# One gate in four of the expert steps moved from VectorE to GpSimd, with two passes of ScalarE to prepare it

## The reference, cut to what matters

```
xn = layernorm(x)                                     # x: 4096 rows of 256
s  = state_space_block(xn)                            # conv, silu, scan over the 4096 rows, 128 x 64 states
tok_w = softmax over the 2 best of 8 experts, per row
g, u = xn @ w1[e], xn @ w3[e]                         # 256 -> 1024, per expert e
hid  = silu(g) * u
out  = sum over the 2 chosen experts of tok_w * (hid @ w2[e])     # 1024 -> 256
y    = x + s * silu(out)
```

## Time and profile before

| | |
|---|---|
| time, median of 3 runs | 1337.58 us (1336.42 to 1339.75) |
| the profiled execution's own time | 1342.63 us |
| its span | 1340.8 us |
| pair loop, first to last scan | 124.4 us to about 1299.8 us of the span |
| busy: TensorE, VectorE, GpSimd, ScalarE | 89%, 87%, 80%, 56% of the span |
| mean granted TensorE clock | 0.945 of full speed |

### The profile page before, as it was taken

One profiled execution on the slowest core, in us unless ns is written; L12 is line 12 of the kernel. 1 busy time (PEld: TensorE's weight loads), 2 busy tenths in 40 slices (PEclk: granted clock), 3 DMA queues, 4 the chain that ended last, 5 costly groups with the idle time before them and its releaser, 6 DMA issues.

```text
span 1340.8 us, 26192 instructions
## 1 busy us (share of the span) xinstructions
PE 1194.0 (89%) x7740; PEld 921.7 (69%) x7740; DVE 1168.6 (87%) x1675; ACT 756.1 (56%) x1619; POOL 1076.3 (80%) x1042
## 2 busy tenths in 40 slices
PE   6788999999999999998999998998899988999760
PEld 5455777777777777776777776876677867777530
DVE  7795989988899989897899888997888988999988
ACT  3754675556554665466555754556455664545642
POOL 0043889888998988888998897898888987989994
PEclk8889999999999999999999999999999999999655
DMA  7124446553557445643574457443754456465658
GB/s 230 52 86 119 135 134 174 169 193 121 161 148 222 134 145 161 220 138 112 168 234 130 135 161 224 135 130 112 214 171 134 132 171 209 142 181 177 181 184 282
DMA packets 124319, 216.55 MB, mean 162 GB/s; under 512 B 15040, under 2 KB 40768, under 8 KB 124160
## 3 DMA queue, kind: packets, MB, share of 16 engines
q10 hardware_dynamic: 73728, 134.25, 34.4%
q1 hardware_dynamic: 43616, 61.83, 14.0%
q0 software_dynamic: 6816, 18.62, 4.4%
HBM read 190.67 MB, written 23.99 MB: 160 GB/s over the span
## 4 chain that ended last, share of the span: by engine, by line
PE 60%; POOL 11%; DVE 10%; issue 8%; DMA 6%; ACT 3%; SPq 1%; ACTq 1%; DVEq 0%; POOLq 0%
PE bank L1323 28%; PE bank L1293 13%; PE bank L1271 7%; PE bank L1339 6%; POOL arena L440 5%; DMA wring<-in_w_all 4%; POOL hid L455 2%; DVE arena L1045 2%; ACT th L720 1%; PE bank L1173 1%; DVE arena L983 1%; PE bank L1198 1%; DVE arena L1036 1%; PE bank L1306 1%; DVE arena L871 1%
## 5 line engine op out<-in xcount | busy, mean ns | idle before, releaser
L440 POOL TENSOR_TENSOR arena<-arena,c_rep 128x512 f32<-128x512 f32 x512 | 604.3, 1186 | 109.3 <-DVE arena L1045 97.8
L1045 DVE TENSOR_TENSOR_SCAN arena<-bank,carry,arena 128x512 f32<-128x512 f32 x512 | 653.1, 1276 | 16.7 <-ACT bank L807 16.5
L1323 PEld LDWEIGHTS bank<-xgT,wring 128*128 128x128 f32 x4288 | 524.4, 196 | 122.8 <-issue 78.4
L1323 PE MATMUL bank<-xgT,wring 128*128 128x128 f32 x4288 | 544.3, 281 | 42.4 <-DMA wring<-in_w_all 18.4
L807 ACT ACTIVATE bank<-arena,a_neg 128x512 f32<-128x512 f32 x512 | 354.8, 693 | 103.1 <-DVE arena L1045 41.1
L1036 DVE TENSOR_TENSOR arena<-bank,b_rep 128x512 f32<-128x512 f32 x512 | 352.4, 688 | 32.1 <-PE bank L1339 10.5
L720 ACT ACTIVATE th<-bank 128x256 f32<-128x256 f32 x284 | 109.1, 384 | 346.7 <-PE bank L1323 321.3
L1293 PE MATMUL bank<-wring,hid 128*128 128x256 f32 x1072 | 273.0, 386 | 15.9 <-POOL hid L455 15.8
L1339 PE MATMUL bank<-stack,pick 128*128 128x512 f32 x512 | 273.3, 538 | 8.4 <-DVE arena L1036 8.4
L1293 PEld LDWEIGHTS bank<-wring,hid 128*128 128x128 f32 x1072 | 194.4, 191 | 74.9 <-POOL hid L455 34.6
L455 POOL TENSOR_TENSOR hid<-gt,ue 128x256 f32<-128x256 f32 x284 | 207.1, 729 | 21.5 <-DVE gt L1057 16.4
(11 more groups left out here) (181 smaller groups left out, 760.4 us busy)
## 6 DMA issues: line engine op xcount, KB each, us to landing
arena<-delta_d ACTq DMA_DIRECT2D x512, 256.0 KB, 3.7
wring<-in_w_all SPq DMA_DIRECT2D x64, 384.0 KB, 6.0
xn<-in_x SPq DMA_DIRECT2D x4, 1024.0 KB, 9.6
xn_d<-xn SPq DMA_DIRECT2D x4, 1024.0 KB, 4.7
parts_d<-spare SPq DMA_DIRECT2D x16, 256.0 KB, 4.1
stack<-parts_d SPq DMA_DIRECT2D x16, 256.0 KB, 6.2
wring<-results SPq DMA_DIRECT2D x8, 512.0 KB, 8.1
arena<-results SPq DMA_DIRECT2D x8, 512.0 KB, 8.5
```

The costliest lines, as they stand in the source:

```text
L440: pool.tensor_tensor(p_ring[:, s % P_RING, :], h_ring[:, s % H_RING, :], of_chunk(c_rep, c, 2), ALU.mult).then_inc(s_hc, 1)
L1045: v.tensor_tensor_scan(out=h_ring[:, s % H_RING, :], data0=a_bank[s % 2][:, :], data1=b_ring[:, s % B_RING, :], initial=carry[:, q:q + 1], ...
L1323: ins = pe.matmul(bank[:, m * SW + r * SLOT:m * SW + (r + 1) * SLOT], wring[:, 2 * j + r, (2 * m + h) * P:(2 * m + h + 1) * P], xgT[:, i % ...
```

## The change

The fourth step of every tile (`POOLED` = 3; 71 of the 284 steps) gets its gate from GpSimd. GpSimd can't read the PSUM bank here, so ScalarE first writes two things to SBUF behind its tanh and copy: the gate half of the bank, copied into `gt`, and tanh + 1, written over `th` in place. Then it raises `s_gc`. GpSimd waits for `s_gc`, multiplies `th` and `gt` into `gt`, raises `s_gp`, and, after waiting for its own result, makes `hid` as before. VectorE skips this step's gate. ScalarE's next tanh (the next tile's first step) now waits for `s_gp`, and TensorE's reuse of the bank waits for `s_gc`.

```diff
+POOLED = STEPS - 1
+        def gated(eng, k):
+            if k % STEPS == POOLED:
+                eng.wait_ge(s_gp, k // STEPS + 1)
+            else:
+                eng.wait_ge(s_gt, (STEPS - 1) * (k // STEPS) + k % STEPS + 1)
...
             def hidden(i, j):
                 k = STEPS * i + j
-                pool.wait_ge(s_gt, k + 1)
+                if j == POOLED:
+                    pool.wait_ge(s_gc, i + 1)
+                    pool.tensor_tensor(gt[:, k % 2, :], th[:, :], gt[:, k % 2, :], ALU.mult).then_inc(s_gp, 1)
+                gated(pool, k)
                 pool.wait_ge(s_ue, k + 1)
...
                 act.wait_ge(s_gu, k + 1)
-                ge(act, s_gt, k)
+                if k:
+                    gated(act, k - 1)
                 act.activation(th[:, :], bank[:, 0:SW], ACT.Tanh, scale=0.5).then_inc(s_th, 1)
                 ge(act, s_hid, k - 1)
                 act.activation(ue[:, k % 2, :], bank[:, SW:2 * SW], ACT.Copy).then_inc(s_ue, 1)
+                if j == POOLED:
+                    act.activation(gt[:, k % 2, :], bank[:, 0:SW], ACT.Copy)
+                    act.wait_ge(s_th, k + 1)
+                    act.activation(th[:, :], th[:, :], ACT.Identity, bias=1.0).then_inc(s_gc, 1)
...
-                    if turn == "step":
+                    if turn == "step" and j != POOLED:
                         k = STEPS * i + j
                         v.wait_ge(s_th, k + 1)
...
                 if kind == "step":
-                    pe.wait_ge(s_gt, STEPS * t + k + 1)
+                    if k == POOLED:
+                        pe.wait_ge(s_gc, t + 1)
+                    else:
+                        gated(pe, STEPS * t + k)
```

More of the change, by code:

```diff
@@ L285, in mamba_and_experts @@
         s_gu, s_xgT, s_th, s_gt, s_ue, s_hid = (sem(k) for k in ("s_gu", "s_xgT", "s_th", "s_gt", "s_ue", "s_hid"))
-        s_o, s_oev = sem("s_o"), sem("s_oev")
+        s_o, s_oev, s_gc, s_gp = sem("s_o"), sem("s_oev"), sem("s_gc"), sem("s_gp")
         s_res = sem("s_res")
```

## The result

The changed kernel takes 1375.57 us (1373.82 to 1377.44), the kernel before 1338.66 us beside it: ratio 1.0276, 95% interval 1.0258 to 1.0294, or 36.9 us slower. The sign was forecast, the size was not: 11 us were expected, and the time lies above the stated range. The profiled execution took 1374.88 us, with a span of 1373.1 us.

A forecast was written before the change was run, and what follows sets the result against it. It took the chain that ended last, 60% TensorE and 11% GpSimd, as deciding what counts. Terms -6.0 + 11.5 + 4.6 + 1.0 = +11.1 us on 1337.6 gave 1348.7 us, range 1333 to 1361.

The forecast's parts named there:

- What bounds the kernel: Whole loop: three engines busy 80% or more; the chain that ended last, 60% TensorE, says how much freed time counts.
- VectorE's relief brings 6.0 us.: VectorE's gate at 13 of 71 fourth steps is in the chain; removing it saves 6.0 us.
- the seven places where TensorE waited for the bank: Fourth steps where TensorE waits for the bank the gate reads: 0 to 0.8 us saved each, 4.1 us together.
- The sign that was set down for VectorE being late more often: In the changed profile: TensorE's waits for VectorE's gate shrinking by clearly more than 6 us.
- GpSimd pays 11.5 us.: Where GpSimd carries the chain, 14 of 71 fourth steps, `hid` comes 0.82 us later: 11.5 us more.
- TensorE pays 4.6 us.: Weight loads of fourth steps' second products wait for the later `hid` at 23 of 67 live tiles: 4.6 us more.
- ScalarE pays 1.0 us.: ScalarE's two extra passes: 0.5 us for the next pair's later Exp, 0.5 us for the next tanh's new wait.
- The new wait of the tanh: Next tile's first tanh waits for GpSimd's gate at 17 of 70 tiles: 13.3 us in sum, 0.5 us counted.
- The stall at the tanh: Rival: the tanh's 13.3 us are paid too, as the late Exp stalls the scans; about 1362 us, chance 0.10.
- the absorption by GpSimd's idle time: Rival: GpSimd's idle time takes the new product, only VectorE's 6.0 us saving stays; 1331.6 us, chance 0.17.
- the shared port: Rival: each new GpSimd product holds up VectorE, 51.8 us more; about 1389 us, chance 0.03.
- The draw: Rival: half of GpSimd's places pay (5.7 us), TensorE's waits hide, VectorE's 6.0 us stay; 1337.3 us, chance 0.20.

The follow-up runs named there:

- the relief alone: The kernel before without VectorE's gate at every fourth step, nobody making it (`hid` is the square of the up half): 1336.33 us, ratio 0.9997.
- the two own-buffer runs: ScalarE writes tanh + 1 into a separate buffer: in the changed kernel 1374.85 us; in that kernel with the second step pooled instead of the fourth 1360.06 us.
- the two product runs: The kernel before with one more GpSimd product at every fourth step: ahead of `hid`, which waits for it, 1365.78 us; directly behind `hid` 1353.94 us.
- the run with the product behind `hid`: The kernel before with one more GpSimd product, on constant operands, directly behind the fourth step's `hid`: 1353.94 us, ratio 1.0111.

## Why the prediction was wrong, point by point

- **What bounds the kernel.** Right that relieving VectorE brings next to nothing, and that idle time of GpSimd is no free place. Wrong to read cost from where the chain ran: a chain shows one path, and at first steps the data that came second was often only tenths of a microsecond earlier.
- **"VectorE's relief brings 6.0 us."** Measured 1.3 us, not to be told from none. At the seven places where TensorE waited for the bank it needs `xgT` too, and the working left that out. In the prediction's own example, of which it has TensorE start 0.8 us earlier than 267.00, ScalarE's list has

```profile
266.34 0.36 ACT L712 ACTIVATE xgT<-bank 128x256 f32<-128x256 f32 x1
```

  so `xgT` is there at 266.70, and 0.2 us could be gained. The sign that was set down for VectorE being late more often did come (waits of weight loads for its gate fell from 34.0 to 10.3 us), but it doesn't mean that: many of these waits had ended with `xgT` all along and were only put down to the gate, and the relief alone brought nothing.
- **"GpSimd pays 11.5 us."** 13 to 15 us with a product that is shorter (606 ns, and no product that waits for it). The kind of cost was right, the size a little low. It is felt at the next tile's first `hid` (12 us of idle time more ahead of its second product), which had not been looked at; that 14 places of 0.82 us come near it is in part luck.
- **"TensorE pays 4.6 us."** 14 us (28.2 less 14.1). The sum over the 23 tiles was 14.7 us before it was cut: first to the 9.3 us outside GpSimd's runs, then by half. Neither cut is borne out. The term was mis-sized by a factor of three, and its upper bound was too low. That the uncut sum comes so near may be luck; nothing tests it.
- **"ScalarE pays 1.0 us."** This is the step that failed, and the largest miss: 16.3 us, of which the larger part (8.6 to 10.4 us) is `xgT`. The prediction listed the Exp, the issue of the load and the next tanh as standing behind the new passes. It left out the eviction of the next tile's rows, which stands on the very next pair and has its reader waiting. The hint was in the trace, in order of time: 22 first steps begin 0.07 us after that eviction. The list of waits hid it, since it puts 18 of these stops down to VectorE's gate. The price of the later Exp, which was watched instead, could not be seen: with the passes behind it nothing was given back.
- **The new wait of the tanh** was sized about right, at half a microsecond for 13 to 30 us of waiting (0.7 us measured, with noise of over 2). The reason given for it was not: GpSimd is not several pairs behind the scans. In the kernel before its product starts 0.2 to 2.4 us after the scan's end, as means over 16 pairs, and at most 4.8: about two pairs.
- **The rivals.** The stall at the tanh fell with the two own-buffer runs, the absorption by GpSimd's idle time with the two product runs. No scan got longer (1274 ns mean after, 1276 before), nor did the `mult` (688 and 688) or the gates (407 and 406), so nothing of the shared port shows. The draw fell with the result. The price given for the port, 1389 us, left out the forecast's own 11.1 us; nothing hangs on it now.

Open: why the parts sum to 43 us and the change to 37, where the 6 to 8 us of ScalarE's passes behind the eviction go, and what the stops of 0.84 us are.

## What to carry to other kernels

Before work is moved, list for each engine that gets some the next few instructions behind the place, and look up for every one of them how long its reader already waits; a reader that starts within 0.1 us of its data has no room, whether or not the chain goes through it (here two passes of ScalarE cost 16 us of 1338). Removing a wait is different from adding one: where an instruction waits for two things that are about equally late, taking one away can bring nothing (0.9997 and 0.9992 alone, 0.9882 together), while making one of them later cost at once (`xgT`, 1.0111). On an instruction with several semaphores the list of waits can name the wrong engine, or none ("issue"): compare the end of the wait with the ends of everything that the instruction needs before working with the name.

## What the runs showed of the hardware that was not expected

GpSimd's product is faster when both inputs are one buffer: 606 ns here, 610 ns where `ue` is squared, against 723 to 729 ns for two buffers of the same shape. From the run with the product behind `hid`:

```profile
L459 POOL TENSOR_TENSOR thp<-bdn 128x256 f32<-128x256 f32 x71 | 43.1, 606 | 0.0
```

That both are faster for having one buffer as both inputs is the reading; no run changed that alone.

ScalarE's passes over 256 columns from SBUF to SBUF took 401 to 429 ns (three runs), its copies of the same size from a PSUM bank 369 to 392. The functions differ as well (an added constant in the first, none in the second), so the buffer is not shown to be the reason.

On GpSimd a product that waits for the one before it starts 78 ns after that has ended, at all 71 places in three runs; products that don't wait overlap in the records by up to 60 ns.
